# GpSimd drains at four places on its way through a token tower: behind the second norm's roots, behind thirteen block gathers, behind the eleventh and the fifteenth accumulating store

## The reference

```
h = W.T[x]                                     # embedding rows
h = h + attn(layernorm(h))                     # a recurrence: s = tanh(s A' + x B'), then C, a gate, Wo
h = h + ffn(layernorm(h))
ffn: logits = xf gate'; wts, idx = top_k(logits, 1)     # one expert of 8 per token
     y = expert_idx(xf)                        # w2( silu(w1 x) * (w3 x) ), inner width 512
     y = y + gelu(xf sw1') sw2'                # a shared expert for every token
```

## Time and profile before

| | us |
|---|---|
| median of 3 runs | 192.59 |
| lowest, highest | 192.10, 193.27 |
| the profiled execution's own time | 192.78 |
| its span | 191.0 |

### The profile page before, as it was taken

How to read it: one execution, slowest core, us unless ns; L and a number is a source line. 1 busy time by engine, 2 the same in 40 slices (tenths; PEclk the granted TensorE clock), 3 DMA queues, 4 the chain that set the end, 5 groups by cost and what they waited for, 6 DMA issues and landing times.

```text
span 191.0 us, 3176 instructions
## 1 busy us (share of the span) xinstructions
PE 144.2 (75%) x998; PEld 102.9 (54%) x998; DVE 137.1 (72%) x364; ACT 91.5 (48%) x199; POOL 84.3 (44%) x80
## 2 busy tenths in 40 slices
PE   0148889888988879895665987768999999999500
PEld 0127678665665657673222665645766676776400
DVE  0266565999599974998689999727887888887610
ACT  2001212333369943575898666047656466664200
POOL 4788865600000000424000077235588888885750
PEclk9999999999999987999999999999999999999965
DMA  5653538991000000021100012331133233433230
GB/s 147 183 169 101 151 97 251 316 394 52 0 0 2 3 0 3 3 106 57 55 3 2 0 45 96 119 101 31 23 49 38 48 37 37 40 37 42 24 35 0
DMA packets 9955, 13.83 MB, mean 72 GB/s; under 512 B 1936, under 2 KB 4752, under 8 KB 9936
## 3 DMA queue, kind: packets, MB, share of 16 engines
q1 hardware_dynamic: 5904, 9.91, 15.5%
q0 software_dynamic: 4032, 3.67, 12.3%
HBM read 10.17 MB, written 3.41 MB: 71 GB/s over the span
## 4 chain that ended last, share of the span: by engine, by line
PE 41%; DVE 19%; ACT 16%; POOL 13%; issue 7%; DMA 1%; ACTq 0%; POOLq 0%
PE bank L594 12%; PE bank L434 8%; POOL emb_rows L342 8%; PE bank L619 7%; ACT states L634 5%; DVE w_sb L892 4%; PE bank L607 4%; DVE w_hl L824 3%; ACT w_hl L644 3%; POOL rstd L350 2%; PE bank L432 2%; ACT w_hl L646 2%; PE bank L537 2%; DVE stats L747 2%; POOL rstd L361 2%
## 5 line engine op out<-in xcount | busy, mean ns | idle before, releaser
L634 ACT ACTIVATE states<-bank 128x128 f32<-128x128 f32 x56 | 15.5, 277 | 43.5 <-PE bank L434 43.5
L379 POOL DMA_INDIRECT out<-out_blk,row_of x20 | 31.4, 1570 | 9.9 <-DVE out_blk L1026 5.6
L434 PE MATMUL bank<-states,sq_sb 128*128 128x128 f32 x112 | 29.9, 354 | 5.4
L594 PE MATMUL bank<-w_hl,xblk_t 128*128 x120 | 29.1, 379 | 0.9 <-issue 0.9
L434 PEld LDWEIGHTS bank<-states,sq_sb 128*128 128x128 f32 x112 | 19.7, 219 | 14.1 <-ACT states L634 14.0
L361 POOL TENSOR_TENSOR rstd<-vareps,cst 128x2 f32<-128x2 f32 x8 | 5.5, 691 | 48.8 <-DVE vareps L753 48.8
L432 PE MATMUL bank<-x_in,sq_sb 128*128 128x128 f32 x112 | 25.6, 315 | 1.3 <-issue 0.7
L372 POOL DMA_INDIRECT w_sb<-x_rows,row_in x16 | 16.6, 1034 | 11.9 <-PE bank L573 8.2
L432 PEld LDWEIGHTS bank<-x_in,sq_sb 128*128 128x128 f32 x112 | 20.1, 225 | 1.9 <-issue 1.7
L714 ACT ACTIVATE w_sb<-bank,factor 128x512 f32<-128x512 f32 x20 | 13.7, 687 | 13.3 <-PE bank L594 11.8
L1000 DVE SCALAR_TENSOR_TENSOR w_sb<-bank,factor,w_sb 128x512 f32<-128x512 f32 x20 | 15.0, 749 | 5.8 <-ACT w_sb L714 4.8
(11 more groups left out here) (132 smaller groups left out, 267.6 us busy)
## 6 DMA issues: line engine op xcount, KB each, us to landing
w_sb<-w SPq DMA_DIRECT2D x24, 256.0 KB, 6.5
x_rows<-norm SPq DMA_DIRECT2D x4, 256.0 KB, 2.3
out<-attn_out SPq DMA_DIRECT2D x4, 256.0 KB
sw_sb<-sw SPq DMA_DIRECT2D x2, 256.0 KB
cst<-consts SPq DMA_DIRECT2D x1, 420.0 KB
sq_sb<-sq SPq DMA_DIRECT2D x1, 384.0 KB
out<-out_blk,row_of POOLq DMA_INDIRECT x20
emb_rows<-emb,tok_sb POOLq DMA_INDIRECT x16
```

The lines of the kernel that those rows point to most:

```text
L379: pool.indirect_dma_start(out=out, out_offset=bass.IndirectOffsetOnAxis(ap=row_of[:, k:k + 1], axis=0), in_=out_blk[k % RING][:], in_offse ...
L434: pe.matmul(pre, at, states[:, i * COLS:(i + 1) * COLS], start=False, stop=True).then_inc(pre_ready, 1)
L594: mm = pe.matmul(hb[:], xblk_t[:, k % 3, b * P:(b + 1) * P], w[:, bass.ds(e * INNER + a * EXPERTS * INNER, INNER)], start=(j == 0), stop=( ...
L634: act.activation(states[:, (i + 1) * COLS:(i + 2) * COLS], bank[i % 2][:, 0:COLS], ACT.Tanh).then_inc(state_ready, 1)
```

## The change

`drain()` is an instruction on GpSimd's stream. Four are added and nothing is removed or reordered: drain 1 behind the eight roots of the second norm, drain 2 behind the thirteen gathers and ahead of the read of `few_blocks`, drain 3 behind store k = 10 and drain 4 behind store k = 14 (and ahead of the two branches). The drain that ends the block was there before.

```
+DRAIN_AT = (10, 14)
...
                 pool.wait_ge(var2_ready, n + 1)
                 pool.tensor_tensor(rstd2[:, ts], vareps2[:, ts], cst[:, C_POW:C_POW + 2], ALU.pow
                                    ).then_inc(rstd2_ready, 1)
+            pool.drain()
             pool.wait_ge(x_stored, 16 * GROUPS)
...
                     pool.wait_ge(blk_turned, k - BESIDE - 3)
                 take_block(k)
+            pool.drain()
             pool.wait_ge(experts_ready, 1)
             few = pool.value_load(few_blocks[0:1, 0:1], min_val=0, max_val=1)
...
                 add_block(k)
                 if AHEAD + k < FEW:
                     take_block(AHEAD + k)
+                if k in DRAIN_AT:
+                    pool.drain()
```

## The result

| | before | changed |
|---|---|---|
| median | 192.82 us (4 runs) | 195.58 us (4 runs, 194.74 to 196.74) |
| ratio, with its 95% interval | | 1.017 (1.012 to 1.022) |
| profiled execution: time, span | 192.78, 191.0 us | 196.74, 194.9 us |
| the block's own drain on GpSimd | 4.64 us | 0.46 us |

The change makes the kernel slower by some 2.8 us. The forecast was 192.6, no change, with a range up to 195.4. Ratios leave out executions more than 1.5% above the fastest of their series: one of 194.33 us in a series of the kernel before, and 196.46 and 196.64 us in the series with drain 2 behind the read.

A forecast was written before the change was run, and what follows sets the result against it. The end was taken as bound by GpSimd's 4.64 us final drain. Added drains cost 1.4 + 2.2 + 2.4, less 2.1 absorbed, 3.9 us; less 4.07 at the tail gives -0.2 on 192.78: 192.6 us, range 190.2 to 195.4.

The forecast's parts named there:

- What bounds the end, and the tail: GpSimd's final drain clears 56 indirect-DMA entries at 0.08 us each; with 5 left it takes 0.57 us, 4.07 less.
- Rival 3: The drain at the program's end stays 4.6 us, so the 3.9 us of lateness remain: 196.7 us, chance 0.06.
- Drain 1: Behind the last root, its 16 entries take 1.5 us inside 18.6 us of GpSimd idle time: cost nothing.
- A drain waits for the landing: An added GpSimd drain must wait for the newest transfer to land, some 1.7 us after a store's instruction ends.
- rival 1: GpSimd's drain looks at the engine and not at transfers, the walk following at once: 190.7 us, chance 0.24.
- It walks old entries while the newest is in flight, and ends when that one lands.: In drains 2 to 4, clearing old entries at 0.08 us each is hidden under the newest transfer's landing.
- Rival 2: All entries are cleared only after the newest has landed, 2.8 us more over drains 2 to 4: 195.4, chance 0.14.
- Restart: GpSimd's next indirect DMA behind a drain starts 0.8 us later, with 0.3 as the lower bound.
- The absorbed idle time, 2.1 us: Between stores 14 and 19 GpSimd waited 2.1 us for VectorE, so that much lateness is made up.
- Drain 4: Behind store 14, four entries: 4.05 us plus 0.2 for two branches against a 1.86 step, 2.4 us more.
- the touches at tenths: Late stores delay VectorE's buffers for blocks 11, 15 and 19 by tenths at most, at no cost to TensorE.

The follow-up runs named there:

- the drains in idle time: Kernel before with only drain 1 and a drain behind the eighth gather added: 191.51 us against 192.57, ratio 0.994.
- the second profile: The changed kernel profiled again with nothing edited: profiled execution 194.80 us, series median 194.81 us against 192.55 before, ratio 1.012.

## Why the prediction was wrong, point by point

- **What bounds the end, and the tail.** Right. The long drain goes by the number of entries: 0.46, 0.79, 2.27, 2.67, 3.33 and 4.64 us for 5, 9, 27, 32, 40 and 56, that is 0.05 + 0.082 n. The forecast had 4.07 us less at the end; it was 4.18. Rival 3 is out. The fixed part, taken as 0.17 from the first drain, is 0.05.
- **Drain 1.** Right: free. It ended at 91.40, 1.4 us behind the last root (16 entries).
- **A drain waits for the landing.** Right against rival 1: in the changed kernel none ended before the landing ahead of it, and the rule of the Trainium skill (PSUM — Partial Sum Buffer, "Engine vs sequencer instructions": a drain waits for the engine to go fully idle) is true here and not enough: on GpSimd it waits for the transfer as well.
- **"It walks old entries while the newest is in flight, and ends when that one lands."** This is the step that failed, in its second half. After the landing all entries cost 0.041 us once more: 0.57, 0.77 and 0.20 us behind the landings of drains 2, 3 and 4 (13, 18 and 4 entries), 1.5 in all. Rival 2 had the right side but twice the size. Its time, 195.4, comes close to the 195.58 by luck: it charged 2.8 us for the walk where 1.5 were paid, and the two terms below made up the rest.
- **Restart.** 0.72 us behind drain 3, for 0.8 taken, and 0.99 behind drain 4 with the two branches, for 0.8 + 0.2. Behind drain 2 it was 1.2 beside the read's 0.8: the first store 2.7 late in place of 1.4. In the kernel with drain 2 alone it was 0.8. The extra 0.4 comes with two added drains ahead of the first store, even where neither is at work then (see the drains in idle time); its cause is open.
- **The absorbed idle time, 2.1 us.** The second term that was mis-sized. It came from one profiled execution, in which VectorE had fallen behind by 0.9 us; that of drain 1 alone leaves 1.3.
- **Drain 4.** 2.65 us over the normal step in the second profile (2.4 forecast), and 4.4 in the first, with the late sixteenth.
- **VectorE.** I had the touches at tenths. Store 5 landed late (by one sixteenth again, at 159.29, with an instruction packet at 156.7 ahead of it), and block 9 waited 1.96 us for its buffer. In the changed kernel it cost nothing at the end, since the stores themselves had become the bound; with drain 2 alone it did (see there).

Three terms make up nearly all of the miss: the second pass 1.5 us, the idle time that wasn't there 0.8, the longer restart behind drain 2 0.4. None of them alone would have turned the forecast into the measured time. The sum by these values, for the second profile: drain 2 about 2.5, drain 3 2.95, drain 4 2.65, less 1.3 made up, is 6.8 us at the last store; its trace has 188.87 - 134.94 = 53.9 us from the first `out_blk` to the last store against 47.2 in the kernel with drain 1 alone, 6.7. Less the 4.18 of the tail that is +2.6, and the two measured series gave +2.8 and +2.3.

The expected gain did not vanish: all 4.2 us arrived at the end. What was lost is that GpSimd was behind VectorE by 0.4 to 5 us over all of stores 0 to 14, and a drain in a queue that is behind costs its landing, its second pass and its restart in full.

## What to carry to other kernels

Indirect DMAs leave entries behind that the last drain of the program has to clear, 0.08 us each here: look in the trace for the sequencer's records behind the last transfer, since the chain of waits stops short of them. Clear them where the issuing engine is idle anyway and has nothing in flight, or put one drain in front of the final waits so that up to half of the walk goes under the last landing; not in the middle of a queue that is behind. And size what can be "made up" from more than one profiled execution.

## What the runs showed of the hardware

- A GpSimd drain with its newest indirect DMA still in flight ended at max(end of that DMA on POOL + 0.05 + 0.041 n, landing) + 0.041 n us: all 20 such drains of these traces, from n = 4 to 56, within 0.05 us. One that began after everything had landed took 0.05 + 0.082 n us (12 drains, n = 4 to 56, within 0.02). What the two passes are isn't shown.
- The sequencer begins a drain up to three stores early (162.1 for one that waits for a store issued at 166.5), so its recorded duration (8.5 us) is not its cost (3.0 us).
- One sixteenth of a store landed 1.8 us behind the other fifteen, with a 16 KB instruction packet of 0.9 us just ahead of it. In the kernel before such late parts cost nothing; here drain 4 waited for it, and with it all of GpSimd.
- The view of idle times named VectorE as the releaser of stores that a drain had held.
